# Attention in a fused transformer block: score maxima turned by quarters, some of them taken before the attention begins

## The reference

```python
q_lat = (x @ Wq_down).reshape(b, t, H, L)      # k_lat, v_lat alike; H = 16, L = 64
q = jnp.concatenate([q_c, _apply_rope(q_e, cos, sin)], axis=-1)   # 16 a head, k alike
scores = jnp.einsum('bhqd,bhkd->bhqk', q, k) * scale
scores = jnp.where(causal[None, None], scores, -jnp.inf)
att = jax.nn.softmax(scores, axis=-1)
y = jnp.einsum('bhqk,bhkd->bhqd', att, v)
```

## Time and profile before

| | |
|---|---|
| median of 3 runs | 2733.7 us (2732.51 to 2735.7) |
| profiled execution | 2731.9 us, span of its instructions 2730.0 us |
| projection | to 283.3 us |
| attention | 283.3 to about 2003 us |
| routing and experts | from there to 2730.0 us |
| busy over the span | PE 92%, DVE 70%, ACT 61%, POOL 27% |

### The profile page before, as it was taken

The page is one execution under the profiler, slowest core; times in us unless marked ns, Lnnn a source line. Parts: engine busy times, 40 slices in busy tenths (PEclk is TensorE's granted clock), DMA queues, the critical chain, the costliest instruction groups (busy, mean ns, idle before and its releaser), DMA issues. The chain is left out here.

```text
span 2730.0 us, 46770 instructions
## 1 busy us (share of the span) xinstructions
PE 2522.9 (92%) x16092; PEld 1304.6 (48%) x16093; DVE 1904.2 (70%) x3194; ACT 1669.5 (61%) x2989; POOL 745.8 (27%) x694
## 2 busy tenths in 40 slices
PE   6986799999999999999999999999957669999998
PEld 4553233333333333333333333333236559989997
DVE  5986788888888888888888888887035656556543
ACT  1665027777777777777777777777833345545544
POOL 2445300110110110110110110110114747766644
PEclk8998569999999999999999999999978779999999
DMA  5797911523532532532532531400057647557565
GB/s 172 212 255 218 138 49 36 103 41 94 103 43 69 103 45 67 103 44 68 104 46 66 103 47 38 76 14 10 17 154 219 199 159 136 115 107 130 98 96 77
DMA packets 214886, 271.22 MB, mean 99 GB/s; under 512 B 27280, under 2 KB 176304, under 8 KB 212272
## 3 DMA queue, kind: packets, MB, share of 16 engines
q1 hardware_dynamic: 175408, 221.01, 36.8%
q0 software_dynamic: 32160, 41.57, 8.8%
q10 hardware_dynamic: 7136, 6.32, 0.7%
HBM read 136.30 MB, written 131.74 MB: 98 GB/s over the span
## 5 line engine op out<-in xcount | busy, mean ns | idle before, releaser
L1074 DVE TENSOR_REDUCE mxc<-ps 128x2 f32<-128x1024 f32 (+4 forms) x1168 | 1297.8, 1148 | 295.1 <-PE ps L982 182.7
L1055 ACT ACTIVATE probs<-ps 128x512 f32<-128x512 f32 (+1 forms) x2240 | 1184.3, 588 | 401.9 <-PE ps L1012 372.0
L1012 PE MATMUL ps<-qs,ks 99*128 99x512 bf16 (+3 forms) x2560 | 736.8, 351 | 6.5 <-ACT probs L1055 4.5
L982 PE MATMUL ps<-ks,qs 96*128 96x512 bf16 (+3 forms) x2560 | 696.8, 362 | 46.9 <-PEq L262 33.8
L1028 PE MATMUL ps<-probs,vs 128*32 128x512 f32 (+3 forms) x5120 | 600.0, 541 | 1.2 <-issue 0.5
L1012 PEld LDWEIGHTS ps<-qs,ks 99*128 99x128 bf16 x2560 | 216.2, 97 | 606.6 <-ACT probs L1055 461.2
L939 POOL TENSOR_SCALAR_AFFINE_SELECT probs<-probs 128x512 f32<-128x512 f32 x256 | 162.2, 634 | 993.5 <-ACT probs L1055 993.5
L982 PEld LDWEIGHTS ps<-ks,qs 96*128 96x128 bf16 x2560 | 240.8, 99 | 260.7 <-DVE mxc L1074 62.0
L1675 PEld LDWEIGHTS ps<-x_t,w_at 128*128 128x128 f32 x2000 | 247.2, 195 | 11.7 <-issue 5.5
L1675 PE MATMUL ps<-x_t,w_at 128*128 128x128 f32 x2000 | 249.0, 279 | 4.0 <-ACT x_t L1716 4.0
L1799 POOL DMA_INDIRECT out<-ys,idx x122 | 195.2, 1600 | 173.4 <-DMA out<-ys,idx 92.2
(11 more groups left out here) (172 smaller groups left out, 1816.9 us busy)
## 6 DMA issues: line engine op xcount, KB each, us to landing
ks<-k_parts SPq DMA_DIRECT2D x96, 256.0 KB, 13.2
qs<-q_parts SPq DMA_DIRECT2D x96, 256.0 KB, 15.2
xs<-slot_x SPq DMA_DIRECT2D x128, 131.0 KB, 2.2
v_ones<-vout SPq DMA_DIRECT2D x64, 256.0 KB, 3.6
vs<-v_ones SPq DMA_DIRECT2D x16, 1024.0 KB, 26.4
attn_t<-o_sb SPq DMA_DIRECT2D x64, 256.0 KB, 3.5
slot_x<-zero SPq DMA_DIRECT2D x24, 655.0 KB, 9.2
q_parts<-parts SPq DMA_DIRECT2D x96, 128.0 KB, 2.5
```

The costliest lines, as they stand in the source:

```text
L982: ins = pe.matmul(o[:, h, :], qs[r][0:SROWS, h0 + h, i * P:(i + 1) * P], ks[r][0:SROWS, h0 + h, 512 * c:512 * c + w], start=first, stop=no ...
L1012: ins = pe.matmul(o[:, h, :], ks[r][0:SROWS + MROWS, h0 + h, j * P:(j + 1) * P], qs[r][0:SROWS + MROWS, h0 + h, J * QJ + lo:(J + 1) * QJ], ...
L1055: act.activation(probs[:, (NKT * r + m) % NPB, h0:h0 + nh, 0:QJ - lo], st_view(r, s), ACT.Exp, scale=DH ** -0.5).then_inc(exp_done, 1)
L1074: dve.tensor_reduce(mxc[:, h0:h0 + nh, i, c], red_view(u, at), AX_X, ALU.max).then_inc(red_done, 1)
```

## The change

- The final maxima, the split, the turn and the rows are made per quarter q of a group, four times in place of once. A turn is one transpose of [128, 48] in place of three of [128, 64], and the rows of a quarter are four DMAs (one a head).
- The scores of quarter J wait for the rows of quarter J only.
- The planner has a job of its own for each turn, and also writes VectorE's stream and the orders of GpSimd (splits and masks) and SyncE (rows and stores), sorted by planned time. The fixed places (six units, the split before the last masks) are gone.
- The first 13 units (`HEAD`, those of i < 6) of group 0 are made at the end of `project`, behind its own work on TensorE and VectorE. The rows of ones are set there once by GpSimd and copied to the two other buffers by DMA in the attention; `mxc` is allocated and set in the projection too.
- The loads at the attention's start are parted: v of group 0, rows of quarter 0, half the loads of group 1, rows of quarter 1, the other half and the ones, rows of quarter 2, then v of group 1, group 2 and the rest.

```diff
@@ project, vector @@
+                dve.memset(g0["mxc"][:, :, :, :], -3e38).then_inc(head_set, 1)
+                dve.wait_ge(ld_small, 16 * 2)
+                dve.tensor_copy(k["mask_qk"][:, :], mask_in[:, :]).then_inc(head_set, 1)
                 staged(dve, (0, normed), (2, rotate), (3, split))
-                dve.wait_ge(ld_small, 16 * 2)
-                dve.tensor_copy(k["mask_qk"][:, :], mask_in[:, :])
+                dve.wait_ge(head_set, 2)
+                for u in range(HEAD):
+                    dve.wait_ge(g0["red_ready"], u + 1)
+                    unit_maxima(dve, g0["mxc"], ps, u, u).then_inc(g0["red_done"], 1)
@@ project, gpsimd @@
+                pool.wait_ge(low_done, 2 * NB + 4)
+                pool.memset(g0["ks"][SROWS:SROWS + MROWS, :, :], 1.0)
@@ project, tensor @@
+                pe.wait_ge(g0["ld"], G_LD)
+                pe.wait_ge(head_set, 2)
+                pe.wait_ge(copy_done, 2 * NB + 2)
+                pe.wait_ge(vcopy_done, NB + 1)
+                for u in range(HEAD):
+                    if u >= NRED:
+                        pe.wait_ge(g0["red_done"], u - NRED + 1)
+                    unit_products(pe, k, ps, g0["ks"], g0["qs"], u, u).then_inc(g0["red_ready"], 1)
@@ planner @@
-                if ok and not (n + 1 < nit and x == self.of_tile[self.first_masked][-1] and n + 1 not in neg):
+                if (n, J) in rows_in and v > tile - self.npb and not (before >= 0 and before % nv in self.last and v <= before):
                     at = exp_end[s - self.nst] + hop if s >= self.nst else 0.0
-                    now.append((max(at, rows_in[n]) if x == 0 else at, "scores", n, x))
+                    now.append((max(at, rows_in[n, J]) if j == 0 else at, "scores", n, x))
+            elif what == "turn":
                 pe = begin + self.TURN_PE
-                dve = max(dve, pe + hop) + self.TURN_DVE
+                dve = max(dve, pe + hop, rows_in.get(turns[t - 1], 0.0) if t > 0 else 0.0) + self.TURN_DVE
+                rows_in[n, x] = dve + self.ROWS
+                sp_events.append((dve, "rows", n, x))
@@ attention, sync @@
+                def maxima(n, q, r):
+                    sp.wait_ge(mt_done, NJ * n + q + 1)
+                    rows = MROWS * KPJ
+                    for h in range(HG):
+                        to = qs[r][SROWS:SROWS + MROWS, h, q * QJ:(q + 1) * QJ].rearrange("m (i t) -> m i t", t=P)
+                        sp.dma_start(to, m_t[rows * h:rows * (h + 1), :]).then_inc(m_ld, 16)
...
+                load_v(0, 0)
+                for what, n, x in course.sp_order:
+                    if what == "out":
+                        output(n, x, n % R)
+                    else:
+                        maxima(n, x, n % R)
+                    if (what, n, x) == ("rows", 0, 0):
+                        for m in range(len(COMBOS) // 2):
+                            load_rows(sp, d, 1, m, ks[1], qs[1], ld[1])
@@ attention, gpsimd @@
+                for what, n, x in course.pool_order:
+                    if what == "split":
+                        split(n, x)
+                    else:
+                        if (n, x) == (1, DIAG[-KPJ]):
+                            weights()
+                        mask(n, (NKT * n + x) % NPB, x)
@@ attention, tensor @@
-                def turn(n, at):
-
-                    pe.wait_ge(part_step, PART * n + PART)
+                def turn(n, q, at):
+
+                    pe.wait_ge(part_step, PART * (NJ * n + q + 1))
                     pe.wait_ge(red_done, at - NRED + 1)
                     apart(pe)
-                    for m in range(MROWS):
-                        ins = pe.transpose(o[:, m * P:(m + 1) * P], mparts[:, m, :], k["identb"][:, :])
-                    ins.then_inc(red_ready, 1)
+                    pe.transpose(o[:, 0:P], mparts[:, q, :, :, :].rearrange("p h m i -> p (h m i)"), k["identb"][:, :]).then_inc(red_ready, 1)
@@ attention, tensor, scores @@
+                    if s == 0 and 0 < n < R:
+                        pe.wait_ge(ones_ld, 16 * (R - 1))
+                    if h0 == 0 and j == 0:
+                        pe.wait_ge(m_ld, M_LD * (NJ * n + J + 1) + 1)
@@ attention, vector @@
+                def turn(n, q, at):
+
+                    dve.wait_ge(m_ld, M_LD * (NJ * n + q) + 1)
                     dve.wait_ge(red_ready, at + 1)
+                    o = red_ps[0:MROWS * QUARTER, at % NRED, 0, :].bitcast(BF16)
+                    dve.tensor_copy(m_t[:, :], o[:, 0:P]).then_inc(red_done, 1)
```

More of the change, by code:

```diff
@@ L651, in order @@
         share = np.concatenate([[0], np.cumsum(cost)]) / sum(cost)
+        turns = [(n, q) for n in range(nit) for q in range(self.nj)]
+        last_unit = {units[u][3]: u for u in range(nu)}
         pe, act, dve, pool, kind = 0.0, 0.0, 0.0, 0.0, None
-        exp_end, red_end, values_end, out_end, ready, rows_in, neg, parts, loaded = [], [], {}, {}, {}, {}, {}, {}, {}
-        order, s, v, g = [], 0, 0, 0
-        first_turn = next(at for at, (_, u) in enumerate(self.stream) if u == turn_unit)
@@ L656, in order @@
[L656 to L667, removed]
+        exp_end, values_end, out_end, ready, rows_in, parts, loaded = [], {}, {}, {}, {}, {}, {}
@@ new lines, in plan, with job @@
+        stream += [(0, u) for u in range(self.head)]
+        red_end = [0.0] * self.head
+        sp_events, s, v, t, g = [], 0, 0, 0, self.head
+        def job(at, what, n, x):
+            nonlocal pool
+            pool = max(pool, at + hop) + (self.SPLIT if what == "split" else self.AFFINE)
+            self.pool_order.append((what, n, x))
+            return pool
+        for q in range(self.nj):
+            if last_unit[q] < self.head:
+                parts[0, q] = job(self.QUARTER_MAX, "split", 0, q)
@@ new lines, in plan @@
+        while s < ns * nit or v < nv * nit or g < nu * nit or t < len(turns):
+            now, at = [], red_end[-self.nred] + hop if len(red_end) >= self.nred else 0.0
+            if g < nu * nit:
+                n, u = divmod(g, nu)
+                q = units[u][3]
+                ok = n * per_group + work[u] <= (1 + s // ns + (share[s % ns] if s < ns * nit else 0) + self.RUN_AHEAD) * per_group
+                if u == last_unit[q] and n > 0:
+                    ok = ok and t > self.nj * (n - 1) + q
+                if n >= 3 and u == 0:
@@ L668, in order @@
                     ok = ok and n in loaded
-                    at = max(at, loaded.get(n, 0.0))
                 if ok:
-                    now.append((at, "unit", n, u))
+                    now.append((max(at, loaded.get(n, 0.0)) if u == 0 else at, "unit", n, u))
+            if t < len(turns) and turns[t] in parts:
+                now.append((max(at, parts[turns[t]] + hop), "turn") + turns[t])
             if s < ns * nit:
                 n, x = divmod(s, ns)
-                tile = n * nv + sets[x][0]
+                m = sets[x][0]
+                J, j, _ = tiles[m]
+                tile = n * nv + m
@@ L703, in order @@
                         out_end[before // nv * self.nj + tiles[before % nv][0]] = act
+                        sp_events.append((act, "out", before // nv, tiles[before % nv][0]))
                     if tile >= self.npb:
@@ L708, in order @@
                 if x == self.of_tile[m][-1]:
[L709 to L715, removed]
+                    ready[tile] = job(act, "mask", n, m) if m in self.diag else act
                 s += 1
@@ L732, in order @@
                 red_end.append(dve)
[L733 to L737, removed]
-                g += 1
-        return order
+                stream.append((n, x))
+                q = units[x][3]
+                if x == last_unit[q]:
+                    dve += self.QUARTER_MAX
+                    parts[n, q] = job(dve, "split", n, q)
+                g += 1
+        self.end = max(pe, act)
+        self.sp_order = [e[1:] for e in sorted(sp_events)]
+        for J in range(self.nj):
+            if ("out", nit - 1, J) not in self.sp_order:
+                self.sp_order.append(("out", nit - 1, J))
 def attention(nc, a, d, k, ps, g0, retired):
@@ L972, in group @@
                 def group(n, u, at):
[L974 to L975 removed]
+                    r = n % R
                     if u == 0:
```

261 lines of the change are left out of this document (122 added, 139 removed).

## The result

The changed kernel takes 3163.95 us (median of 4 runs, 3154.47 to 3169.17) against 2733.11 us: a ratio of 1.157, interval 1.154 to 1.160. It is 431 us slower, where 2692 was predicted and at most 2722 allowed. The profiled execution spans 3158.7 us.

The account below looks back on a forecast made before the run. TensorE was taken to bound the middle, but not the fill or tail. Gains of 46 and 6 less losses of 8 and 2 made 42 us off 2731.9, so 2689.9; adding 1.8 for the median, 2692, range 2668 to 2722.

Parts of the forecast that it names:

- The reading of the kernel before: Whole attention: TensorE bounds the middle at 102.1 us a group, not the ends; the fill loses 66 us of its time.
- (a) Quarters: Fill: scores start after one quarter's rows, at 291; TensorE loses 20 us instead of 66, a gain of 46 us.
- R1: Fill: TensorE waits briefly again and again, the clock swings, 15 to 30 us more lost; 2707 to 2722; chance 0.17.
- (b) Head: Start of the attention: 13 units, 5.8 us of TensorE work, hide in the projection; a gain of 6 us.
- (c) Turns: Every group: four turns for one cost TensorE 0.5 us a group, 8 us over sixteen groups.
- (d) GpSimd's order: Every group: three more splits of at most 1.4 us on GpSimd fit into its gaps; nothing extra.
- (e) SyncE's order: SyncE's queue: rows behind loads have some 5 us margin, costing nothing in a steady group; 2 us allowed in group 1.
- The signs: Profile after: wrong if period over 104.7 us, VectorE waiting for rows each group, half clock past 320, or start after 284.
- R2: Loading groups: quarter 0's rows behind loads hold VectorE, 20 us in each of 13 groups; 2950, mild 2745; chance 0.10.
- all slower cases: Whole kernel: any result slower than the kernel before, given a chance of 0.10.
- both ends together: Fill and start of the attention: predicted gains of 46 us from quarters and 6 us from the head.
- the middle: Steady groups: predicted loss of 8 us, from four turns in place of one at 0.5 us a group.

Follow-up runs that it names:

- repaired kernel: The changed kernel with reciprocals at unit 20 instead of 56 and loads put behind the next rows in SyncE's order: 2697.7 us, 0.987 of the kernel before.
- the run with the loads moved: The changed kernel with the loads of group n+3 behind the next rows in SyncE's order, reciprocals still at unit 56: 2885.0 us.

## Why the prediction was wrong, point by point

**The reading of the kernel before** held: a fill that loses 66 us of TensorE's time (by instruction counts 67), and a middle bound by TensorE at 102.

**(a) Quarters.** First scores at 291.6, predicted 291. Quarter 3 of the first group came at 379.9 instead of 366. Its last final maximum was at 370.6 and not near 358: I had put the gaps between VectorE's 60 units at 2.5 us, and they were 18.5 us, all of them waits for TensorE's products, while TensorE worked on scores as well and ran at half clock for 31 of the 88 us. The loss in the fill, reckoned as in the prediction, is 31 us and not 20. The clock rose at 303.7, as predicted (about 300), but did not stay. Stretches of the fill in the kernel after (columns as in the windows above):

```profile
304.00:331.00 27.00, 24.97 (x175) 8.49 (x167) 23.66 (x23) 14.35 (x28) 3.39 (x8) 1.00 0.56 73
331.00:341.00 10.00, 8.99 (x27) 3.32 (x28) 7.14 (x8) 3.26 (x6) 0.00 (x0) 0.50 0.54 144
342.00:375.00 33.00, 31.00 (x216) 11.31 (x215) 26.71 (x28) 19.63 (x38) 3.39 (x8) 1.00 1.04 180
376.00:389.00 13.00, 11.31 (x36) 4.03 (x40) 8.33 (x9) 6.33 (x12) 0.84 (x4) 0.50 0.15 39
```

It was at 0.50 again from 331 to 341 and from 376 to 389. These are the stretches around the turns of quarters 2 and 3, in which the scores of one quarter were used up and the next quarter's rows had not come. TensorE fed units there and stopped now and then before a turn or a unit; for rows it waited once, for 2.6 us. The repaired kernel waited longer there, for 9.1 us in three waits, and its clock was at 0.50 three times (309.8 to 313.2, 337.1 to 343.9, 378.0 to 395.1). The swing of the clock that R1 expected is in these rows; in the kernel before there was none, the clock stayed at 0.50 from 254.0 to 389.8. This is R1 in a mild form, by the mechanism that R1 named, with 11 us more lost instead of 15 to 30.

**(b) Head.** It hid as said: the last head unit ended at 278.9 (predicted 279.5), the attention began at 282.6. Its worth is about 12 us by the attention's end and not 5.8. The term was TensorE's work; the number says that at the fill's start VectorE's 13.2 us count for more.

**(c) Turns.** Predicted +0.5 us a group; the repaired kernel has 102.73 against 102.04, +0.7. The idle time of the earlier trace rows, which I took for TensorE's, is that of its weight loads: in a steady group its matmuls fill the whole time, before (102.00 us) and in the repaired kernel. It was also not the size of the wait: four turns idle 2.5 us of weight-load time a group, 0.63 each, where one idled 0.19. So this wait lies under running matmuls, and the 0.7 us include whatever else the new order changes in a group.

**(d) GpSimd's order** cost nothing that shows.

**(e) SyncE's order** is the step that failed. I wrote that rows behind the loads have a margin of some 5 us, "so it costs nothing in a steady group". The forecast has it at nothing in a steady group; it cost 36.9 us in each. Three things were wrong in it.
- I measured the margin to VectorE's next copy and not to TensorE's scores, because I took from the kernel before that the maxima of a group lie nearly a whole group ahead. The diff removes the condition that enforced this (scores behind the first diagonal tile wait for the next group's maxima), and RUN_AHEAD is only an upper limit. In the new order the rows of quarter 2 are turned at 552.0 for scores at 568.4: 16 us of slack against a landing time of 26 us behind loads, which stood in the earlier trace rows (29 us here). The planner could not see it: it gives the rows 4.0 us from VectorE's copy, whatever stands ahead of them on SyncE, and they took 53.6.
- I did not walk SyncE's queue. The store of quarter 3 is followed by a wait for the reciprocals of the group before, taken at unit 56 of the next group. With the maxima a whole group ahead that unit is long past when the store is issued. With half a group of lead it was 23 us away (545.6 to 568.2).
- The two add up, because the wait delays the loads and the rows together. 36.9 us in each of eleven periods are 406, the step into the third group adds 40, and the last two groups, which load nothing, 7.8 each. The two ends give back 32 us (15.4 later at the second group's last maximum; 46.1 us from the last maximum to the end instead of 93.6). Together that is +430, the attention's end at 2425.7 against 1996.0. Of the 15.4 us at the second group's last maximum 10.4 are a wait for rows behind loads (issued at 437.6, there at 464.1), for which I had allowed 2 us.

**The signs.** The period (138.9, over the 104.7 that I had named) and the half clock behind 320 us (331 to 341) showed the forecast wrong. The start of the attention (282.6) did not, and VectorE never waited for rows: TensorE did.

**The rivals.** R2 had the kind of mechanism, rows behind loads, but for quarter 0's rows and with VectorE waiting. In the changed kernel it was quarter 2's rows and TensorE. R2 took place as written only in the run with the condition put back. Ten per cent for all slower cases was too little for a change that rewrites the orders of SyncE and GpSimd.

**The page's rule** (the Trainium skill, DMA: Bandwidth & Descriptors, "Queues, rings and completion order"), that completion is not in order of issue on one engine's queue, is no promise that a small DMA overtakes. In the changed kernel the DMA issued just ahead of the rows landed at 605.0 and the wait for the rows ended at 605.6. Even with the loads on another queue the waits for rows ended 6.4 to 19.2 us after their issue.

**What the repaired kernel gains,** 30 us of attention, checks the remaining terms: both ends together 39.7 us (52 predicted), the middle -9.5 (-8 predicted, with no stall in it). A small part of it is a gain that I had not listed. With less lead, the stretch after the last maxima, in which ScalarE is the busiest engine, is 44.8 us long instead of 93.6, and TensorE is busy for 39.3 of it instead of 85.8 of 93.6: it stands idle for 5.5 us and not for 7.9.

## What to carry to other kernels

When a change loosens the order between engines, ask first how far ahead each producer really runs afterwards; a limit in a planner is not a lead. Then walk the written order of every engine that the change touches, instruction by instruction, and set each wait and each bulk transfer against the slack of whatever stands behind it. And when two delays stand in one queue, repair both before judging the change: each alone left some 14 us a group here, both together none.

## What the runs showed of the hardware

- Issuing a DMA soon after many others can hold the issuing engine. Three fills issued 4 us after the last load held SyncE for 22.4 us in the run with the loads moved. In the kernel before, the same three issues took 4.5 us at 522 us, 21 us after the last load. Why, no run shows.
- A DMA issued behind the loads of a group landed 26 to 29 us later, whether it carried 256 or 512 KB. With the loads on a second queue a store still took 15.8 and 20.0 us. The DMA share was 1.04 and 1.05 while they were in flight, and 1.00 from 574.0 to 605.6 in the rows below. That all queues share the DMA engines is the likely reason; it is argued, not tested.
- TensorE's clock, from the stop at 568.4 in the third group of the kernel after:

```profile
568.40:574.00 5.60, 0.04 (x4) 0.00 (x0) 1.40 (x2) 0.00 (x0) 0.00 (x0) 0.94 0.77 108
574.00:605.60 31.60, 0.00 (x0) 0.00 (x1) 0.00 (x0) 0.00 (x0) 0.00 (x0) 0.50 1.00 173
605.60:611.00 5.40, 5.40 (x19) 1.56 (x20) 1.87 (x2) 2.44 (x5) 0.00 (x0) 0.51 0.00 0
611.00:620.00 9.00, 9.00 (x60) 3.06 (x62) 7.66 (x8) 7.87 (x16) 0.00 (x0) 1.00 0.50 168
```

It was 0.50 from 574 on, stayed so for the first 5 us after TensorE was busy again, and was 1.00 by 611. In the kernel before it took 8 us, in the fill of the repaired kernel 10 us (385.2 to 395.1). Behind the eleven stalls of 33 us it came back 3.4 to 13.4 us after TensorE did. So each stall also costs half speed for the first microseconds behind it.
